# A four-pass graph kernel: GpSimd waits for the landing of one group's indirect DMAs ahead of issuing the next group's

## The reference

```python
x = _layernorm(x + _L0_gnn_ref(x, edge_index, edge_type_4, ...))                 # attention by edge type
x = _layernorm(x + _L1_gnn_ref(x, edge_index, edge_attr_64, ...))                # message MLP, segment_sum
x = _layernorm(x + _L2_gnn_ref(x, L2_gnn_global_context, ..., node_type_3, src, dst))   # 8-head attention
x = _layernorm(x + _L3_gnn_ref(x, edge_weight, src, dst))                        # weighted segment_sum
```

```python
gathered = vals[:, None] * x[cols]
return jax.ops.segment_sum(gathered, rows, num_segments=n)
```

## Time and profile before

| | |
|---|---|
| time, median of 3 runs | 3320.36 us (3319.99 to 3322.48) |
| span of the profiled execution | 3278.8 us |
| time of a run less that span | 41.6 us |
| TensorE busy | 2119.1 us, 65% |
| VectorE busy | 1616.3 us, 49% |
| GpSimd busy | 1686.9 us, 51% |
| ScalarE busy | 1177.9 us, 36% |
| mean granted TensorE clock | 0.653 of full |

### The profile page before, as it was taken

The page is one execution under the profiler, slowest core; times in us unless marked ns, Lnnn a source line. Parts: engine busy times, 40 slices in busy tenths (PEclk is TensorE's granted clock), DMA queues, the critical chain, the costliest instruction groups (busy, mean ns, idle before and its releaser), DMA issues. The chain is left out here.

```text
span 3278.8 us, 39377 instructions
## 1 busy us (share of the span) xinstructions
PE 2119.1 (65%) x9903; PEld 1708.7 (52%) x9903; DVE 1616.3 (49%) x4408; ACT 1177.9 (36%) x3337; POOL 1686.9 (51%) x1704
## 2 busy tenths in 40 slices
PE   5335676879783778888772175766577755555467
PEld 2225565757662667667651165655555433333367
DVE  3236777776841234423331144566577754444356
ACT  2245555555421223333221144444445322222234
POOL 3466655565104556666615545656545666666600
PEclk9655555555556889899885555555557775666579
DMA  6544434343103223232214333334332222222255
GB/s 233 204 132 125 121 102 118 108 126 106 44 9 86 65 66 83 67 82 69 80 36 118 89 102 108 110 112 118 107 88 65 74 69 69 68 74 68 67 190 173
DMA packets 244607, 322.35 MB, mean 98 GB/s; under 512 B 105346, under 2 KB 160931, under 8 KB 243045
## 3 DMA queue, kind: packets, MB, share of 16 engines
q0 software_dynamic: 66560, 163.90, 17.5%
q1 hardware_dynamic: 177797, 155.67, 15.6%
HBM read 257.60 MB, written 63.38 MB: 98 GB/s over the span
## 5 line engine op out<-in xcount | busy, mean ns | idle before, releaser
L1318 POOL DMA_INDIRECT e_gathered<-msg_src_table,src_idx x416 | 398.9, 959 | 422.0 <-POOLq L364 165.6
L692 POOL DMA_INDIRECT e_gathered<-rel_src_table,rel_idx x416 | 431.1, 1036 | 344.4 <-ACT e_gathered L891 145.2
L1866 POOL DMA_INDIRECT e_kv<-kv_table,src_idx x416 | 406.0, 976 | 368.9 <-DVE e_weighted L2236 164.1
L1879 POOL DMA_INDIRECT rows_by_src<-e_kv,e_row x416 | 425.4, 1022 | 260.4 <-DVE e_kv L2165 131.0
L1953 PE MATMUL e_ps_q<-e_window,e_spread 64*128 64x128 f32 x1664 | 350.7, 380 | 218.7 <-issue 125.2
L1953 PEld LDWEIGHTS e_ps_q<-e_window,e_spread 64*128 64x128 f32 x1664 | 308.0, 277 | 293.2 <-issue 281.7
L2088 ACT ACTIVATE e_spread<-e_offsets,e_minus_lane 64x512 f32<-64x512 f32 x208 | 149.1, 717 | 673.0 <-remote 389.6
L750 PE MATMUL e_ps_r<-e_window,e_spread 64*128 64x128 f32 x832 | 211.2, 429 | 178.8 <-DMA e_window<-rel_dst_table 104.4
L750 PEld LDWEIGHTS e_ps_r<-e_window,e_spread 64*128 64x128 f32 x832 | 181.7, 319 | 207.8 <-DMA e_window<-rel_dst_table 135.0
L1988 PE MATMUL e_ps_a<-e_onehot,e_weighted 128*128 128x66 f32 x832 | 190.5, 401 | 146.9 <-DVE e_weighted L2236 88.0
L1988 PEld LDWEIGHTS e_ps_a<-e_onehot,e_weighted 128*128 128x128 f32 x832 | 171.5, 304 | 170.6 <-DVE e_weighted L2236 121.2
(11 more groups left out here) (445 smaller groups left out, 4301.4 us busy)
## 6 DMA issues: line engine op xcount, KB each, us to landing
n_rows<-rows_by_src SPq DMA_DIRECT2D x26, 1032.0 KB
e_offsets<-group_offsets SPq DMA_DIRECT2D x208, 128.0 KB
e_keys<-tile_keys SPq DMA_DIRECT2D x104, 128.0 KB
e_window<-rel_dst_table SPq DMA_DIRECT2D x416, 32.0 KB
e_mixed<-in_edge_attr_dram SPq DMA_DIRECT2D x103, 128.0 KB
rel_src_table<-t_up SPq DMA_DIRECT2D x5, 2560.0 KB
e_gathered<-rel_src_table,rel_idx POOLq DMA_INDIRECT x416
e_gathered<-msg_src_table,src_idx POOLq DMA_INDIRECT x416
```

The lines of the kernel that those rows point to most:

```text
L692: pool.indirect_dma_start(gathered[:, q % GS, j, :], None, rel_table, bass.IndirectOffsetOnAxis(ap=rel_idx[:, q * J + j:q * J + j + 1], ax ...
L1318: pool.indirect_dma_start(gathered[:, q % GS, j, :], None, msg_table, bass.IndirectOffsetOnAxis(ap=src_idx[:, q * J + j:q * J + j + 1], ax ...
L1866: pool.indirect_dma_start(kv[:, q % RING, j, :], None, kv_table, bass.IndirectOffsetOnAxis(ap=src_idx[:, q * J + j:q * J + j + 1], axis=0) ...
L1879: pool.indirect_dma_start(in_order, bass.IndirectOffsetOnAxis(ap=row[:, q // 2 % RS, q % 2 * J + j:q % 2 * J + j + 1], axis=0), kv[:, slot ...
```

## The change

Ahead of each group's four indirect DMAs GpSimd now also waits until the four of the group before have landed. The count is 16 for each DMA, times four, times the number of uses that this slot's semaphore has had. Nothing else is changed, no instruction moves, and the rings keep their sizes.

```diff
             def pool_program(pool):
                 for q in range(Q):
                     hold(pool, reduced, q - GS + 1)
+                    if q:
+                        pool.wait_ge(src_in[(q - 1) % GS], 16 * J * ((q - 1) // GS + 1))
                     pool.nop(nofuse=True)
                     for j in range(J):
                         pool.indirect_dma_start(gathered[:, q % GS, j, :], None, rel_table,
...
                     hold(pool, h_mm, q - GS + 1)
+                    if q:
+                        pool.wait_ge(src_in[(q - 1) % GS], 16 * J * ((q - 1) // GS + 1))
                     pool.nop(nofuse=True)
...
                     hold(pool, weighed, q - RING + 1)
+                    if q:
+                        pool.wait_ge(src_in[(q - 1) % RING], 16 * J * ((q - 1) // RING + 1))
                     pool.nop(nofuse=True)
...
                     pool.wait_ge(placed, q // 2 + 1)
+                    if q:
+                        pool.wait_ge(sent[(Q + q - 1) % RING], 16 * J * ((q - 1) // RING + 1))
                     pool.nop(nofuse=True)
```

## The result

| | before | changed |
|---|---|---|
| median of 4 runs each, same chip | 3320.18 us (3301.15 to 3322.48) | 3616.89 us (3612.32 to 3620.04) |
| ratio, 95% interval | | 1.092 (1.089 to 1.095) |
| span of the profiled execution | 3278.8 us | 3618.0 us |
| time of that execution less its span | not recorded | 2.0 us |

The changed kernel is 9.2% slower. The prediction was 3506 us, 3425 to 3620: the direction is right and the loss is more than a third too small, 186 against 297 us (339 us from span to span).

What follows compares the result with a forecast made beforehand. GpSimd was taken to set the pace, with gaps of at least landing plus restart: +39, +38, +14 and +70, 161 us, plus 25 for longer waits, on a span of 3278.8, plus 41.6 outside it: 3506 us, range 3425 to 3620.

Steps and rivals of the forecast that it cites:

- The landing sets GpSimd's pace: All four passes: each gap between groups lasts at least landing plus restart; 3506 us, from 3425 to 3590, chance 0.72.
- The issue times: GpSimd's time for a group of four indirect DMAs: 5.04, 4.74, 4.80 and 4.99 us in passes 1 to 4.
- The restart: From a semaphore that becomes true to GpSimd's next record: 0.75 us, used in all passes.
- What the users give back: Passes 1 to 3: users trailing GpSimd's end would trail less, returning 18, 26 and 35 us; pass 4 nothing.
- the size of the landing: Behind the fourth issue's end: 1.8, 1.45, 1.6 and 1.2 us in passes 1 to 4, including 0.2 for the semaphore's update.
- The 25 us for waits that are longer than the landing: Added for waits for slots or data that would still be met; bounds 0 and 50 us.
- the 41.6 us "outside the span": Median of the runs above the profiled span of 3278.8 us, taken as untouched by the change and added.
- the 248 boundaries "with nothing to wait for": Of 412 boundaries between groups before the change, those where GpSimd was taken to run on at once.
- Rival 2: Pass 2: TensorE's clock falls as slower groups keep it less busy; 3605 us at most, 3555 if half, chance 0.07.
- Rival 3: Three gathers: landing behind a stop as slow as at pass 2's end, 2.1 us and 0.2; 3717 us, chance 0.10.
- Rival 5: No change: the added wait hides under waits for slots that are there anyway; 3300 to 3330 us, chance 0.05.
- Rival 4: Faster: pauses end other engines' standstills, as in pass 3, if the mean gap is under 1.87 us; 3250 us, chance 0.06.

Runs made afterwards that it cites:

- the last experiment: Changed kernel with three of SyncE's loads made small after their first round through the buffers: 3529.84 us against 3611.08 of the changed kernel on another chip.

## Why the prediction was right and wrong

**Right.** The landing sets GpSimd's pace at all boundaries: at nearly each of the 412 the next DMA starts 0.73 us (0.87 in pass 4) behind the last landing of the group before, and at none more than 1.2 us. The issue times were 5.04, 4.74, 4.80 and 4.99 us and came out as 5.03, 4.80, 4.93 and 4.91. The restart was 0.75 and came out as 0.73 (0.87 in pass 4). What the users give back was 18, 26, 35 and 0 us; the stretches between the passes shrank by 17.1, 23.1 and 35.3 us, and the end grew by 1.6.

**Wrong, the step that failed: the size of the landing.** It was taken as 1.8, 1.45, 1.6 and 1.2 us behind the fourth issue's end. It is 2.17, 1.73, 2.09 and 1.61 in the mean of the boundaries, so 1.55 us more over the four passes, and 103 x 1.55 = 160 us. The mechanism was right, and both terms of this size were too small, as the changed kernel's trace shows: it holds the packets in which the data moves, and the increments of the semaphore, 16 to a DMA, the last of which ends the wait.

The first term is the traffic. The last packet of GpSimd's queue ends 1.74, 1.36, 1.70 and 1.12 us behind the issue, where 1.6, 1.25, 1.4 and 1.0 were read in the earlier trace rows: 0.67 us, or 69 us of time. Those places were picked because SyncE's queue was quiet there, and that made them exceptions. With 50 of SyncE's 156 MB gone, as in the last experiment, the last packet ends at 1.56, 1.26, 1.49 and 0.94 us, which in sum is what the quiet places gave.

The second term is what follows the last packet. No row showed it, and 0.2 us was put in. From the last packet to the last increment it is 0.43, 0.37, 0.39 and 0.49 us: 0.88 us more over the four passes, or 91 us, and with the 50 MB gone it is 0.34 to 0.47 us.

The landing did not get slower by the change. On the chip with both profiles the last landing of a group comes 2.14, 1.74, 2.11 and 1.67 us behind its fourth issue before and 2.19, 1.69, 2.08 and 1.62 after. A DMA of pass 3 takes 2.9 us from the start of its issue to its landing before (the fence above) and after, by the DMAs that the profile could match, 48 and 104 of 416:

```profile
DMA to landing us min/median/max: 2.7/2.9/4.0
```

The sum had 0.95 + 1.6 = 2.55 us for it. The Trainium skill, "DMA: Bandwidth & Descriptors", section "Anatomy of one DMA — SWDGE (gpsimd) path", gives 2.0 us plus bytes/436e3, from which 2.3 us for a DMA of 128 KB is an estimate. Counted from the issue's start, that is 0.6 us less than these 2.9 us.

**Wrong, two smaller terms.** The 25 us for waits that are longer than the landing were nothing, since the landing was the last wait at every boundary: landing and restart alone make the mean gaps, 2.17 + 0.73 = 2.90 us in pass 1. And the 41.6 us "outside the span" are not there in any execution that has both numbers: 2.0 to 2.1 us lie between time and span. The kernel before was measured at 3301 too, so its profile was most likely of a quicker execution, of some 3281 us. The terms close: 3506 + 160 (landing) + 6 (restart) + 10 (issue) - 25 + 2 (gaps between passes, start and end) - 39.6 = 3619, measured 3620.04 in the execution whose span these terms are read from. A small misreading changed nothing: the 248 boundaries "with nothing to wait for" were counted from waits named "issue", which hold some real ones of up to 2.9 us; at 231 the gap was 0.30 us.

**The rivals.** Rival 2 is refuted, the clock stayed at 0.91. Rival 3 had the landing at 2.3 us in the gathers; the truth, 2.0 us in the mean, lies between its 3717 and the forecast. Rival 5 is refuted. Rival 4's standstills are there, and they and the shorter delays beside them go with the largest difference of all, that between 3320 and 2725 us. But GpSimd issues without a pause on the chips of 2725 us too, so its issuing alone doesn't cause them. The rival lost all the same, since its own condition, a mean gap under 1.87 us, wasn't met at 2.67. The kernel with the empty instruction ahead of the second DMA has 0.30 + 1.63, 0.90 + 0.92, 0.30 + 1.67 and 0.33 + 1.28 us in two gaps where there were two anyway, 1.83 us in the mean less the second's 0.30, so 1.53 and under 1.87, and it is faster by 4.1%.

**What the masked case teaches.** On the chips without standstills the change costs 3611 - 2729 = 882 us, three times as much. The pace of the changed kernel is the same on both; what differs is how much of it the kernel before was already losing: in pass 1, for one, its gaps between groups are 1.94 us in the mean on the first chip and 0.83 us on the other.

**Open.** Why two of the six chips and the first one (which may be one of the two) show standstills isn't settled. Neither is it shown that it is the chip and not the occasion: no chip with standstills was met twice for certain. Neither the issue's duration nor TensorE's differs. A bound of eight DMAs in flight doesn't help. Whether the recording takes part is open, as said above. The three kernels without long standstills on such chips (the changed one, the one with its wait behind the empty instruction, and the one with wait and empty instruction ahead of the second DMA) all pause GpSimd at nearly every group and all bound the DMAs in flight to four or five, so it isn't shown which of the two does it, nor how short a pause would do.

## What to carry to other kernels

A wait for a transfer just issued costs landing plus restart less the work that stands between, when the waiting engine sets the pace: put it one group back, where it was free here, or ahead of the third DMA of the next group, where it cost 0.5%. Take a latency from places with the load that the change will have, not from the quiet ones. Count to the semaphore's increment and not to the last packet, which here left out 0.4 us. And measure on more than one chip before taking a profile's idle time as the kernel's own.

## What the runs showed of the hardware

- One and the same kernel takes 2725 us on some chips (four of the six of these sets) and 3279 to 3320 us on others, with the same durations of single instructions. On the latter the other engines stand still at times while GpSimd issues indirect DMAs with gaps of 0.30 us (TensorE busy 16 of 130 us and not 73), and a semaphore's update was recorded 18.9 us behind the end of the matmuls that made it.
- An indirect DMA that waits itself starts 0.26 us after the landing it waits for; with an empty instruction in between that holds the wait it is 0.73 to 0.87 us.
- The landing of a 128-row DMA of 1 KB rows comes 2.7 to 5.4 us after its issue's start, 2.9 in the median. Behind the last of four such DMAs some 0.2 us are due to other loads (2.17 and 2.09 us against 1.96 and 1.84), and 0.43 and 0.39 us lie between its last packet and the last increment.
